# Attention scores from row tiles of TensorE, scaling on GpSimd, transposes four heads late

## The reference, cut to what matters

```
scores = (q * scale) @ k.T            # 112 x 112 (self) or 112 x 375
scores = mask(scores)                 # self: causal; layers 1, 3: key mask; others: none
p = softmax(scores)                   # exp(s - max) / sum
out = p @ v
```

## Time and profile before

| | us |
|---|---|
| median of 3 runs | 2167.96 (2167.66 to 2169.86) |
| the profiled execution | 2164.93 |
| its span in the trace | 2163.1 |
| TensorE busy, share of the span | 1976.2, 91% |
| VectorE | 1286.9, 59% |
| ScalarE | 917.9, 42% |
| GpSimd | 1185.7, 55% |

### The profile page before, as it was taken

How to read it: one execution, slowest core, us unless ns; L and a number is a source line. 1 busy time by engine, 2 the same in 40 slices (tenths; PEclk the granted TensorE clock), 3 DMA queues, 4 the chain that set the end, 5 groups by cost and what they waited for, 6 DMA issues and landing times.

```text
span 2163.1 us, 35765 instructions
## 1 busy us (share of the span) xinstructions
PE 1976.2 (91%) x12332; PEld 1725.7 (80%) x12332; DVE 1286.9 (59%) x3174; ACT 917.9 (42%) x2326; POOL 1185.7 (55%) x1357
## 2 busy tenths in 40 slices
PE   4998888988899999999999989998879999998998
PEld 3865576777689998989999978996548999987998
DVE  6777766777545254347888845422175888874422
ACT  2025515555421121137777723222134777771321
POOL 3553417557078899966444336870045545423785
PEclk9999889999899999999999999999999999999999
DMA  3110100001023333321000022332230000001232
GB/s 119 39 55 1 38 15 8 15 21 31 22 76 101 116 109 116 115 76 40 9 20 12 12 82 78 108 108 65 77 102 25 20 13 22 13 2 40 88 108 83
DMA packets 38193, 118.88 MB, mean 55 GB/s; under 512 B 6168, under 2 KB 10264, under 8 KB 38016
## 3 DMA queue, kind: packets, MB, share of 16 engines
q1 hardware_dynamic: 31408, 107.92, 16.0%
q10 hardware_dynamic: 6608, 8.68, 1.3%
HBM read 114.75 MB, written 1.84 MB: 54 GB/s over the span
## 4 chain that ended last, share of the span: by engine, by line
PE 57%; DVE 21%; issue 9%; ACT 7%; POOL 4%; DMA 1%; ACTq 0%; DVEq 0%; SPq 0%; POOLq 0%
PE psum L542 9%; PE psum L543 9%; PE psum L544 9%; PE psum L535 6%; PE psum L804 6%; DVE masked_t L1319 4%; PE psum L658 4%; PE psum L660 4%; PE psum L659 4%; DVE kk L1285 3%; ACT probs_t L988 3%; DVE probs_t L1330 3%; PE psum L761 2%; POOL wl L1631 2%; ACT probsT_t L1006 1%
## 5 line engine op out<-in xcount | busy, mean ns | idle before, releaser
L1631 POOL TENSOR_TENSOR wl<-raw,wh 128x256 fp32r<-128x256 f32 x656 | 517.8, 820 | 13.7
L1623 POOL TENSOR_SCALAR wh<-raw 128x1024 fp32r<-128x1024 f32 x164 | 185.4, 1130 | 329.3 <-PE psum L544 181.5
L542 PE MATMUL psum<-nh,wh 128*128 128x448 f32 x904 | 348.6, 386 | 14.5 <-DVEq L1384 7.8
L543 PE MATMUL psum<-nl,wh 128*128 128x448 f32 x904 | 337.7, 374 | 0.0
L544 PE MATMUL psum<-nh,wl 128*128 128x448 f32 x904 | 337.0, 373 | 0.0
L761 PE MATMUL psum<-cst,probs_t 112*125 112x112 f32 (+1 forms) x1304 | 237.9, 280 | 58.0 <-DVE probs_t L1330 57.6
L988 ACT ACTIVATE probs_t<-masked_t,nmin 112x375 f32<-112x375 f32 (+1 forms) x384 | 205.9, 536 | 181.3 <-DVE nmin L1319 178.4
L761 PEld LDWEIGHTS psum<-cst,probs_t 112*125 112x125 f32 (+1 forms) x1304 | 189.4, 183 | 109.8 <-DVE probs_t L1330 106.1
L1330 DVE TENSOR_SCALAR probs_t<-probs_t,rinv 112x376 f32<-112x376 f32 (+1 forms) x520 | 249.9, 481 | 18.5
L1456 DVE TENSOR_TENSOR hid_l<-scr,hid_h 128x448 fp32r<-128x448 f32 x108 | 93.5, 866 | 229.1 <-ACT hid_h L1063 228.5
L542 PEld LDWEIGHTS psum<-nh,wh 128*128 128x128 f32 x904 | 175.5, 194 | 36.6 <-issue 11.1
(11 more groups left out here) (187 smaller groups left out, 4418.5 us busy)
## 6 DMA issues: line engine op xcount, KB each, us to landing
raw<-in_walls SPq DMA_DIRECT2D x183, 512.0 KB, 3.4
raw<-in_ctxF SPq DMA_DIRECT2D x24, 375.0 KB, 3.0
ctxb<-in_ctxF ACTq DMA_DIRECT2D x8, 375.0 KB, 3.9
ctxt<-in_ctxK ACTq DMA_DIRECT2D x8, 375.0 KB
x<-in_xT ACTq DMA_DIRECT2D x2, 896.0 KB, 11.1
outT<-x SPq DMA_DIRECT2D x2, 896.0 KB, 5.0
mask<-in_kmask ACTq DMA_DIRECT2D x16, 41.0 KB, 2.6
vself<-in_tt SPq DMA_DIRECT2D x1, 448.0 KB, 6.7
```

The costliest lines, as they stand in the source:

```text
L542: nc.tensor.matmul(out, ah, bh, start=(i == 0), stop=False)
L543: nc.tensor.matmul(out, ah, bl, start=False, stop=False)
L1631: last = nc.gpsimd.tensor_tensor(low[cut], src[cut], high[cut].bitcast(F32), ALU.subtract)
```

## The change

Three things change together, in all attentions.

1. **Scores.** The masked copies are gone. A matmul takes as its operands only the rows of its head: 32 rows in self-attention (`qT`, `kT` as they are) and in layer 0's cross-attention, 64 rows in layers 1 and 3. Heads are done in pairs on even steps, pass by pass: first pass of head s, first pass of head s + 1, second pass of head s and so on, the two heads in different rows of the array and in different PSUM banks. With split operands there are three passes for each head. The pair waits for `maxed` or `exped` of head s - 1. In layer 0's cross-attention the heads run in the order 0, 2, 1, 3 within each four, and `mcross` lays queries out for even and odd heads alone (four instructions of line 1607 in place of sixteen). `mself` is gone. `split_queries` has two instructions in place of eight, on 128 rows each. The keys of a projection are copied and subtracted with one instruction each in place of two (lines 971 and 1285).
2. **Scaling.** Line 1330 moves from VectorE to GpSimd, as entries "scale" in `WORK`, one per head. Other entries stand at fixed places between them (`scaling`, `keyed`). VectorE's reciprocal moves from one to two steps behind (`BACK` = 2).
3. **Distances.** `LAG` goes from 2 to 4, `NPROB` from 3 to 6. The value projections of layers 1 and 3 come two heads later.

```diff
-LAG = 2
-NPROB = 3
+LAG = 4
+BACK = 2
+NPROB = 6
...
+SCALED = {"S": B * NH, "0": B * NH, "1": B * NH, "2": B, "3": B * NH}
+def scaling(L, between):
+    out = []
+    for s in range(SCALED[L]):
+        out.append((0, "scale" + L, s))
+        out += between.get(s, [])
+    return out
...
+def keyed(L):
+    placed = []
+    for i in range(2, 2 * B):
+        placed.append((8 * i - 9, (0, f"q{L}", i)))
+    for b in range(2, B):
+        placed.append((NH * b - 18, (0, f"ctx{L}", b)))
+    for c, u in enumerate(uses(f"Wo{L}")):
+        placed.append((3 + 12 * c, u))
+    return batches(f"q{L}", 0, 1) + scaling(L, between_of(*placed))
+GU = with_kv1(uses("gu"))
+WORK = (uses("qk") + uses("v") + batches("ctx0", 0, 1) +
+        scaling("S", between_of(*[(118 + 3 * c, u) for c, u in enumerate(uses("dense"))])) +
+        uses("kv0") + uses("cq") + batches("mcross", 0, 1) +
+        scaling("0", between_of(*[(NH * b - 22, u) for b in range(2, B) for u in ((0, "ctx0", b), (0, "mcross", b))],
+                                *[(98 + 6 * c, u) for c, u in enumerate(uses("cdense") + GU[:3])])) +
+        GU[3:] + batches("ctx1", 0, 1) + uses("Wq1") + keyed("1") + uses("kv3") +
+        uses("ff1") + uses("mem") + scaling("2", {}) + uses("memT") + uses("gate") +
+        batches("ctx3", 0, 1) + uses("Wq3") + keyed("3") + uses("ff3"))
...
-            first = {att_c0: -4}.get(a, -1)
-            second = {att_c0: -1}.get(a, 1)
+            first = {att_c0: -4}.get(a, 1)
+            second = {att_c0: -1}.get(a, 3)
...
+        def head_of(a, s):
+            h = s % a.nh
+            return h // 4 * 4 + (0, 2, 1, 3)[h % 4] if a is att_c0 else h
...
                 if s >= 2:
-                    pe.wait_ge(a.maxed if a.mask else a.exped, s - 1)
-                if a is att_c0:
-                    product3(s_bank(s)[:, 0:376], ops).then_inc(a.scored, 1)
-                elif a.k_heads:
-                    product(s_bank(s)[:, 0:376], ops).then_inc(a.scored, 1)
-                else:
-                    product(out, ops).then_inc(a.scored, 1)
+                    pe.wait_ge(a.maxed if a.mask else a.exped, s)
+                wide = a.nk + a.nk % 2
+                passes = [(0, 0), (0, 1), (1, 0)] if a.k_heads else [(0, 0)]
+                for n, (i, j) in enumerate(passes):
+                    for t in (s, s + 1):
+                        h = head_of(a, t)
+                        if a is att_self:
+                            rows = slice(32 * (h % 4), 32 * (h % 4) + 32)
+                            q, k = qT[rows, h // 4, bcols(b)], kT[rows, h // 4, bcols(b)]
+                        elif a is att_c0:
+                            rows = slice(32 * (h % 8 // 2), 32 * (h % 8 // 2) + 32)
+                            q, k = qmx[rows, b % 2, i, h // 8, h % 2, :], keys_of(a, s // 8)[rows, j, :]
+                        else:
+                            rows = slice(64 * (h % 2), 64 * (h % 2) + 64)
+                            q, k = (qd, ql)[i][rows, s // 8 % 2, h // 2 % 4, :], keys_of(a, s // 2)[rows, j, :]
+                        last = nc.tensor.matmul(s_bank(t)[:, 0:wide], q, k, start=(n == 0), stop=(n == len(passes) - 1))
+                        if n == len(passes) - 1:
+                            last.then_inc(a.scored, 1)
...
-                        scores(a, s)
+                        if a is att_2 or s % 2 == 0:
+                            scores(a, s)
...
-                        for h in range(2):
-                            own = slice(64 * h, 64 * h + 64)
-                            last = nc.scalar.copy(keys_of(i)[own, h, :], bank[own, 0:376])
-                        last.then_inc(a.k_high, 1)
+                    nc.scalar.copy(keys_of(a, i)[:, 0, :], bank[:, 0:376]).then_inc(a.k_high, 1)
...
+                own = keys_of(a, i)
+                last = nc.vector.tensor_sub(own[:, 1, :], bank[:, 0:376], own[:, 0, :].bitcast(F32))
...
-                    r = s - 1
+                    r, k = s - BACK, s - 1
...
-                        dve.wait_ge(a.recip, r + 1)
-                        pr = probs[r % NPROB][:, 0:wide]
-                        nc.vector.tensor_scalar(pr, pr, rinv[:, r % NPROB:r % NPROB + 1], None, ALU.mult)\
-                            .then_inc(a.scaled, 1)
...
+                src, high = q1[:, 4 * g:4 * g + 4, bcols(b)], qd[:, i % 2]
+                nc.gpsimd.tensor_scalar(high, src, 1.0, 1.0, ALU.mult, ALU.mult).then_inc(split_h, 1)
+                pool.wait_ge(split_h, n_split + 1)
+                nc.gpsimd.tensor_tensor(ql[:, i % 2], src, high.bitcast(F32), ALU.subtract).then_inc(split_l, 1)
+
+            def scale(a, s):
+
+                pool.wait_ge(a.recip, s + 1)
+                pr, inv = probs[s % NPROB][:, 0:a.nk], rinv[:, s % NPROB:s % NPROB + 1]
+                nc.gpsimd.tensor_scalar(pr, pr, inv, None, ALU.mult).then_inc(a.scaled, 1)
...
+                if b >= 2:
+                    pool.wait_ge(att_c0.scored, NH * (b - 1))
+                work = [(qmx[:, b % 2, i, :, j, :], t[:, :, bcols(b)].bitcast(F32), (C_EVEN, C_ODD)[j])
+                        for j in range(2) for i, t in enumerate((qch, qcl))]
```

More of the change, by code:

```diff
@@ L98, in batches @@
     return [(0, kind, b) for b in bs]
-def per_batch(L):
-    out = []
-    for b in range(2, B):
-        out += [(0, f"q{L}", 2 * b - 2), (0, f"ctx{L}", b), (0, f"q{L}", 2 * b - 1)]
-    return out + batches(f"q{L}", 2 * B - 2, 2 * B - 1)
 def with_kv1(chunks):
@@ L114, in with_kv1 @@
     return out
-WORK = (uses("qk") + batches("mself", 0, 1) + uses("v") + batches("ctx0", 0, 1) +
-        batches("mself", *range(2, B)) + uses("dense") + uses("kv0") + uses("cq") + batches("mcross", 0, 1) +
-        [u for b in range(2, B) for u in ((0, "ctx0", b), (0, "mcross", b))] + uses("cdense") + with_kv1(uses("gu")) +
-        batches("ctx1", 0, 1) + uses("Wq1") + batches("q1", 0, 1) + uses("Wo1") + per_batch(1) + uses("kv3") +
-        uses("ff1") + uses("mem") + uses("memT") + uses("gate") +
-        batches("ctx3", 0, 1) + uses("Wq3") + batches("q3", 0, 1) + uses("Wo3") + per_batch(3) + uses("ff3"))
@@ L126, with between_of @@
-MASKINGS = ("mself", "mcross")
-USES = [u for u in WORK if u[1] not in ("q1", "q3") + MASKINGS]
+SCALED = {"S": B * NH, "0": B * NH, "1": B * NH, "2": B, "3": B * NH}
[5 more added lines that the diff above has]
+    return out
+def between_of(*placed):
+    out = {}
+    for s, u in placed:
+        out.setdefault(s, []).append(u)
+    return out
+def keyed(L):
[7 more added lines that the diff above has]
+    return batches(f"q{L}", 0, 1) + scaling(L, between_of(*placed))
@@ L128 @@
+MASKINGS = ("mcross",)
+USES = [u for u in WORK if u[1] not in ("q1", "q3") + MASKINGS and u[1][:5] != "scale"]
 USES_OF = {name: uses(name) for name in ("kv0", "kv1", "kv3")}
 USE_NO = {u: n for n, u in enumerate(USES)}
-SPLITS = [u for u in WORK if u[1] not in PLAIN and u[1] not in MASKINGS]
+SPLITS = [u for u in WORK if u[1] not in PLAIN and u[1] not in MASKINGS and u[1][:5] != "scale"]
 SPLIT_NO = {u: n for n, u in enumerate(SPLITS)}
@@ L1555, in slot @@
                 return chunk_raw, wh[:, r % RING, :], wl[:, r % RING, :]
-            steps = [0]
             def split_queries(u):
@@ L1568, in split_queries @@
                     pool.wait_ge(ATT[name[-1]].scored, 8 * (i - 1))
-                def step(ins):
-                    steps[0] += 1
-                    ins.then_inc(q_step, 1)
-                    pool.wait_ge(q_step, steps[0])
                 if n_split >= 1:
                     pool.wait_ge(split_l, n_split)
-                for h in range(2):
-                    own, other = slice(64 * h, 64 * h + 64), slice(64 - 64 * h, 128 - 64 * h)
-                    src = q1[own, 4 * g:4 * g + 4, bcols(b)]
-                    step(nc.gpsimd.tensor_scalar(qd[own, i % 2, h], src, 1.0, 1.0, ALU.mult, ALU.mult))
-                    step(nc.gpsimd.tensor_scalar(qd[other, i % 2, h], src, 1.0, 1.0, ALU.mult, ALU.mult))
@@ L1590, in lay_out @@
             def lay_out(u):
                 _, name, b = u
[L1593 to L1605 removed]
+                tile_done(pool, ("cq", b // BPH, 1))
```

90 lines of the change are left out of this document (26 added, 64 removed).

## The result

The changed kernel takes 2212.93 us (2210.18 to 2214.33) against 2167.81: a ratio of 1.0218, 95% interval 1.0194 to 1.0241. The forecast was 2155 with a range of 2105 to 2210; it was wrong in sign and in range.

A forecast was written before the change was run, and what follows sets the result against it. TensorE was taken to bound layers 1 and 3, a loop of latencies self-attention and C0. -16 + 25 - 20 - 2 = -13 us took 2164.93 to 2151.9, and 3 us for the median made 2155; range 2105 to 2210.

The forecast's parts named there:

- Self-attention, -16: Self-attention: 0.85 us per head and a slow end, 120 us against 137.5, 1 back for the next stage's half-clock start.
- C0, +25: Layer 0's cross-attention (C0): a loss of 12 us from pair waits and GpSimd blocks, plus 13 for the clock.
- Half of 3.4 us, for eight such places: 13: Layer 0's cross-attention: TensorE at half clock for 3.4 us after each of eight idle spells, costing 13 us.
- The sum without the clock, +12: Layer 0's cross-attention before the clock term: 8 x 26.6 + 17 + 7 + 5.7 = 242 us against 230.5.
- Rival (b): GpSimd becomes the clock in layer 0's cross-attention, none of its inserted 53 us absorbed: +26 in all, 2194 us; chance 0.15.
- no gain worth counting: Scores in layers 1 and 3: a pair falls from 0.84 to 0.77 us with overlapping row tiles, counted as 0.
- Rival (c): Scores in all attentions: row tiles don't overlap, 2267 us, or overlap in part, 2186; chance 0.13.
- Layers 1 and 3, -10 each: Layers 1 and 3: -18 from less waiting, +7 where GpSimd's blocks meet, +1 for filling.
- 0.74 us of waiting per four heads: Layers 1 and 3: TensorE's waiting, 8.82 - 8.08; 0.55 of it was to go, 32 times: -18 us.
- The meeting at heads 14 and 15: Layers 1 and 3: a context, a split and a weight chunk meet on GpSimd; TensorE loses about 4.2 us.
- Memory attention, -2: Memory attention: scaling leaves its chain, 8 x 0.42 = 3.4 us, partly taken back by the last four context loads.
- Scaling at 1.20: Scaling on GpSimd: 1.20 us for 375 columns, from line 1607's slope; range 0.4 to 1.25.

The follow-up runs named there:

- distances_alone: The kernel before with only the third part of the change (LAG 4, BACK 2, NPROB 6, later values) in all attentions: 2164.8 us, ratio 1.0016.
- self_masked_c0_back: c0_back with self-attention's score pairs over 128 rows from masked copies and its scaling on VectorE: 2146.2 us, ratio 0.9928.
- c0_filler_fit: The changed kernel with matmuls nobody reads, in groups of six and fifteen, in TensorE's idle spells in layer 0's cross-attention: 2177.7 us, ratio 1.0045.
- c0_full_rows: The changed kernel with score passes of layer 0's cross-attention over 128 rows instead of 32, scores not the reference's: 2192.2 us, ratio 1.0112.
- c0_scale_vector: The changed kernel with the scaling of layer 0's cross-attention back on VectorE: 2183.3 us, ratio 1.0088.
- c0_back: The changed kernel with layer 0's cross-attention as before the change, keeping the distance of four and six buffers: 2142.9 us, ratio 0.9890; again 2144.4, 0.9913.
- c0_singles: The changed kernel with scores of layer 0's cross-attention head by head instead of in pairs, waiting for the exponential two before: 2257.3 us, ratio 1.0430.

## Why the prediction was wrong, step by step

- **Self-attention, -16: right.** 0.85 us per head forecast, 0.86 found, 17.6 us less. The slow end too: in the changed kernel transposes wait 3.20 and 2.50 us behind the weight chunks at 240 and 246 us. It gave the pairs no credit by name; distances_alone and self_masked_c0_back show that they made two thirds of the gain.
- **C0, +25: wrong, +67.** The step that failed is "Half of 3.4 us, for eight such places: 13", which puts 27 us of C0 at half clock. It was 147 us, and c0_filler_fit won 37 us back with 31 us still at half clock, so the term is at least 37 and not 13. I took an idle spell of about 2.8 us as the only thing that lowers the clock, since the earlier trace rows shows such a one, and counted one stretch of 3.4 us for each. With passes over 128 rows that would have come near (34 us at half clock in c0_full_rows). Once the passes cover 32 rows, the stage showed a fall after idle spells of 1.4 us and, head by head, after none. Of the terms of the loop, the pair at 3.0 us and the blocks of 6 us with 3.6 idle stood. The sum without the clock, +12, was still too low: in c0_filler_fit, with the clock mostly held, the exponentials of C0 take 256.1 us, 33 more than before. The first six batches, put at 26.6 + 2.8 = 29.4 us each, take 30.6 to 31.5 there, 8 us in all. The last two, 58.5 by the sum (26.6 + 24.9 and 7 for the chunks), take 71.4, in part at half clock; how much of these 13 us is the chunks' own stays open.
- **Rival (b), chance 0.15: the nearest.** It had C0 at +56, the place, the sign and "over 2.0" us per head (2.31). Its mechanism, though, was GpSimd passing its delay on; of the loss that is 28 us by c0_scale_vector, clock included.
- **Row tiles, "no gain worth counting": wrong by a term.** I put a pair in layers 1 and 3 at 0.77, with steps of mode at 0.09 hidden in first passes. It takes 0.71, but with 0.16 more ahead of it and 0.10 more behind. Rival (c) was wrong in its reason (the tiles overlap) and right that row tiles cost: 20 us in layers 1 and 3 and about 10 in self-attention, each against full rows with operands that are not the reference's, and the clock in C0.
- **Layers 1 and 3, -10 each: -0.5 and -1.2.** Two terms failed. Of "0.74 us of waiting per four heads" only 0.35 was idle time in the trace of before (4.9 and 0.7 us in 64 heads); the rest was TensorE's own: four heads' transposes with the step to what follows take 1.26 us, and I had priced them at 0.96. And the pair's 0.13. The meeting at heads 14 and 15 is there: the second batch takes 2.5 to 2.6 us per head against 2.19, 5 to 6 us where 4.2 had been put.
- **Memory attention, -2: 0.** Its exponentials come 3.05 us apart in place of 4.2, but its last value product starts 41.8 us after its first score pass, 41.5 before. The last four groups of value products wait 0.91, 2.18 and 0.76 us for context loads and 0.53 for VectorE, and the last two run at half clock (2.87 us in place of 1.56): the step had named the loads for a part of it and not the clock. A gain of 2 us couldn't be seen here in any case: from this attention's first exponential to that of layer 3 it takes 169.7 to 175.5 us in the runs with this attention as changed.
- **Scaling at 1.20: right**, 1.237 median over 375 columns. What VectorE loses was put at 200 us from medians; line 1330's busy time was 249.9. Nothing in the sum hung on it.

```profile
L1597 POOL TENSOR_SCALAR probs_t<-probs_t,rinv x520: 564/1237/1265, 141.4 to 1995.3; 112x375 f32<-112x375 f32 x131, 112x112 f32<-112x112 f32 x43
```

The Trainium skill, "GPSIMD Engine Reference", section 3.1, puts a tight one-input loop at about 1.8 cycles an element, by an estimate 0.56 us for 375 columns. The trace disagrees, with 1.237 us for this instruction, and the measurement decides.

## What to carry to other kernels

Before narrowing matmuls to the rows that hold data, look at how full the stage keeps TensorE: in C0, a stage bound by latencies, the padded passes held the clock (c0_back: 1.00, 1.77 us per head), and the lean ones ran at 1.2 GHz for half of the time (2.31). Price row tiles as a pair with the way in and out; over 64 rows and 376 columns that came to more than two plain passes each (1.38 against 1.25 us for two heads). In self-attention, where heads wait on a loop of small steps, issuing two at once was worth more than the distance or the change of engine, and an engine that takes over a step in the loop must hold no block longer than the slack.

## What the runs showed of the hardware

- The granted clock of TensorE fell to 0.50 directly behind 10.0 us at full clock in which it was busy without a gap, with passes over 32 rows among them (c0_singles, 421.5 to 431.5).
- With nearly the same idle spells, 1.4 to 3.7 us, passes over 128 rows in place of 32 took the mean clock of C0 from 0.75 to 0.95 (c0_full_rows). Whether the rows do it or the steps of mode that go with them was not measured.
- Matmuls that nobody reads bought time: 51 us of them, 37 us less in all (c0_filler_fit).
- Two heads in row tiles of 64 rows started a few ns apart and took 0.71 us for six passes. The way in cost 0.16 us more ahead of them and the way out 0.10 behind, against the 0.09 that was read for column tiles.
